# Attention of the first stage: probabilities turned in full precision, values as a narrow stationary operand in four column strips, scores in row halves

## The reference, cut to what matters

```python
qp = (q @ Wq + bq).reshape(B, H, S, hd)      # H = 16 heads, hd = 16, q = layernorm(x)
kp = k @ Wk + bk                             # one key and one value head for all 16
vp = v @ Wv + bv                             # k = v = ctx, 77 rows
att = softmax(einsum('bhsd,btd->bhst', qp, kp) / 16)
out = einsum('bhst,btd->bhsd', att, vp)      # back to [B, S, 256]
x = x + tanh(g) * out
```

## Time and profile before

| | us |
|---|---|
| median of 3 runs | 1150.58 (1150.38 to 1151.35) |
| the profiled execution | 1147.46 |
| its span, first to last instruction | 1145.7 |
| mean granted TensorE clock | 0.939 |

### The profile page before, as it was taken

One profiled execution on the slowest core, in us unless ns is written; L12 is line 12 of the kernel. 1 busy time (PEld: TensorE's weight loads), 2 busy tenths in 40 slices (PEclk: granted clock), 3 DMA queues, 4 the chain that ended last, 5 costly groups with the idle time before them and its releaser, 6 DMA issues. The chain is left out here.

```text
span 1145.7 us, 24403 instructions
## 1 busy us (share of the span) xinstructions
PE 981.6 (86%) x7085; PEld 868.5 (76%) x7085; DVE 855.9 (75%) x2301; ACT 588.9 (51%) x1349; POOL 489.0 (43%) x695
## 2 busy tenths in 40 slices
PE   5889989989998675899999999982779869999973
PEld 3767777777776443799999999972668769999962
DVE  3788998898996343688888888875666747888767
ACT  2577777777776352334343434422545346666520
POOL 3455455455453001345354444433376714444420
PEclk9899999999998776999999999996889989999996
DMA  6674674575560040101011010200333213444357
GB/s 157 148 139 96 141 143 96 122 142 116 112 143 1 0 128 22 49 25 48 24 35 37 24 48 24 93 2 1 101 125 120 89 55 117 125 123 130 106 200 241
DMA packets 85875, 104.44 MB, mean 91 GB/s; under 512 B 15070, under 2 KB 75438, under 8 KB 85808
## 3 DMA queue, kind: packets, MB, share of 16 engines
q1 hardware_dynamic: 77616, 81.91, 28.9%
q0 software_dynamic: 7632, 21.05, 5.1%
q10 hardware_dynamic: 560, 0.66, 0.2%
HBM read 38.50 MB, written 57.62 MB: 84 GB/s over the span
## 5 line engine op out<-in xcount | busy, mean ns | idle before, releaser
L413 POOL TENSOR_TENSOR prob_lo_hi<-prob,prob_lo_hi 128x616 f16<-128x616 f32 x64 | 95.7, 1496 | 126.7 <-ACT prob_lo_hi L491 126.5
L1647 POOL DMA_INDIRECT expert_out<-early_weights,aim x71 | 69.9, 984 | 101.3 <-DVE aim L1976 84.1
L721 PE MATMUL ps_scores<-kblock,qT 128*128 128x308 f32 x256 | 82.8, 448 | 11.1 <-ACT qT L475 5.8
L1638 POOL DMA_INDIRECT sorted_rows<-m_z,slot_i x64 | 72.5, 1133 | 42.4 <-DVE slot_i L1856 24.6
L1185 ACT ACTIVATE f_hidden<-c_hidden,f_b 128x256 f32<-128x256 f32 x128 | 53.7, 471 | 69.3 <-PE c_hidden L1374 69.3
L1372 PE MATMUL c_mlp<-f_w_hi,f_hidden_hi 128*128 128x256 f32 x256 | 80.9, 316 | 3.6 <-DVE f_hidden_lo L1303 3.6
L787 PE MATMUL ps_probT<-ident,prob_lo_hi 128*77 128x128 f32 x512 | 68.9, 279 | 15.4 <-DVE probT L364 12.8
L787 PEld LDWEIGHTS ps_probT<-ident,prob_lo_hi 128*77 128x77 f32 x512 | 59.3, 151 | 28.6 <-DVE probT L364 16.5
L1372 PE MATMUL c_hidden<-y2T_hi,f_w_hi 128*128 128x256 f32 x256 | 77.7, 304 | 0.0
L629 DVE TENSOR_REDUCE mx<-ps_scores 128x8 f32<-128x616 f32 x64 | 50.6, 791 | 32.8 <-PE ps_scores L721 32.8
L1374 PE MATMUL c_hidden<-y2T_hi,f_w_lo 128*128 128x256 f32 x256 | 72.8, 284 | 0.0
(11 more groups left out here) (336 smaller groups left out, 3306.3 us busy)
## 6 DMA issues: line engine op xcount, KB each, us to landing
sorted_rows<-no_row SPq DMA_DIRECT2D x15, 2322.0 KB, 13.4
m_z<-sorted_rows SPq DMA_DIRECT2D x71, 129.0 KB
early_weights<-expert_chunks SPq DMA_DIRECT2D x8, 640.0 KB, 4.2
combT<-combineT_all SPq DMA_DIRECT2D x16, 256.0 KB, 2.3
slT<-slots_all SPq DMA_DIRECT2D x16, 256.0 KB, 2.5
early_weights<-expert_out SPq DMA_DIRECT2D x8, 512.0 KB, 6.3
early_weights<-expert_out POOLq DMA_DIRECT2D x8, 512.0 KB, 6.3
out<-x_all SPq DMA_DIRECT2D x8, 512.0 KB, 3.4
```

The lines of the kernel that those rows point to most:

```text
L413: pool.tensor_tensor(prob2[:, u % 2, :, :, 0], prob[:, u % 2], prob2[:, u % 2, :, :, 1], ALU.subtract).then_inc(lo_done.sem, 1)
L721: return pe.matmul(out, lhsT, rhs, start=start, stop=stop)
L1638: pool.indirect_dma_start(out=sorted_rows[:, :], in_=zn[:, s % 3, t, :], in_offset=None, out_offset=bass.IndirectOffsetOnAxis(ap=slot_i[:, ...
L1647: pool.indirect_dma_start(out=expert_out[:, :], in_=xo[:, i % 3, :], in_offset=None, out_offset=bass.IndirectOffsetOnAxis(ap=aim_i[:, i % ...
```

## The change: what it does

- The probabilities are no longer split. `high_part` and `low_part` go; `turn_p` transposes the fp32 probabilities themselves. `scores_out` now waits for `turn_p` to have read the buffer, where it waited for `low_part`.
- `values` is turned round: the stationary operand is `vstat`, [77, 32] (16 values, a column of ones, 15 of zeros), and a pair of heads with all 256 tokens moves (512 columns, fp32). Four such matmuls put their 32 output rows at partitions 0, 32, 64 and 96 of one bank. There are two steps, of 8 heads each, in the place of four. `v_load` (POOL) adds the bias and fills `vstat`; `v_parts` and `add_bv` go.
- The result stands with the head's values down the partitions, so it is copied out (`values_out`, ACT, two of [128, 512]) and transposed back (`turn_values`, PE, two of four transposes). `out_rec` and `out_scale` (DVE) then read PSUM, once per tile of tokens; `out_sum` goes.
- `scores` uses 64 rows a matmul: the upper half of `qT` with `kblock`'s upper rows, then the lower half with the lower rows. `kblock` has 4 heads of columns (308) in place of 8, with a mask that is made once (`hmask`).
- `kv` streams 77 and 16 columns in place of 128 and 128.
- `probT_out` of unit 0 moves from DVE to ACT (`probT_act`, 0).
- DVE's first waits and the mask's construction ahead of the loop grow by one small POOL operation ([128, 4]).
- `order` is another list; the stages of the steps stay, and `v_load` is in MID.

```diff
-        kblock = sb("kblock", [P, UG, L])
-        vpart = sb("vpart_all", [L, NB, 3, HD + 1], BF16)
+        kblock = sb("kblock", [P, UG // 2, L])
+        vall = sb("v_all", [L, NB, HD])
+        vstat = sb("v_and_one", [L, 2 * HD])
+        turned = sb("values_turned", [P, 2, 512])
...
+        order = [(PRE, "ln1_stats"), (OUT, "probT_act", 3), (OUT, "turn_p", 3), (MID, "scores", 0), (OUT, "values", 0),
+                 (MIX, "turn_xu"), (PRE, "ln1_mean"), (MID, "row_max", 0), (MID, "scores_out", 0), (OUT, "values_out", 0),
+                 (MIX, "xuT_out"), (OUT, "values", 1), (PRE, "ln1_apply"), (MID, "row_max", 1), (MID, "scores", 1),
+                 (MIX, "neg_max"), (OUT, "out_rec", 0), (OUT, "values_out", 1), (MID, "exps", 0), (MIX, "combine"),
+                 (MID, "exps", 1), (MID, "scores_out", 1), (MIX, "dispatch"), (MIX, "combineT_out"), (MIX, "logits"),
+                 (OUT, "turn_values", 0), (OUT, "out_scale", 0), (MIX, "neg_maxT"), (MIX, "logitsT"),
+                 (OUT, "turn_values", 1), (MID, "scores", 2), (OUT, "out_rec", 1), (OUT, "out_scale", 1),
+                 (MIX, "normalise"), (MIX, "disp_scale"), (MID, "probT_act", 0), (MIX, "turn_comb"), (MID, "row_max", 2),
+                 (MID, "scores_out", 2), (OUT, "x1"), (MID, "turn_p", 0), (PRE, "kv"), (MIX, "comb_scale"),
+                 (PRE, "kv_move"), (OUT, "ln2_stats"), (MID, "row_max", 3), (MIX, "turn_disp"), (MID, "scores", 3),
+                 (MIX, "disp_out"), (MID, "exps", 2), (OUT, "ln2_mean"), (MID, "turn_p", 1), (MID, "probT_act", 1),
+                 (PRE, "zT_out"), (PRE, "turn_z"), (MID, "scores_out", 3), (OUT, "ln2_center"), (MID, "exps", 3),
+                 (MIX, "slots_out"), (MIX, "slot_inputs"), (OUT, "squares"), (PRE, "rstd1"), (PRE, "q_out"), (OUT, "unit"),
+                 (OUT, "ln2_scale"), (MID, "turn_p", 2), (MID, "probT_out", 2), (OUT, "rstd2"), (MID, "v_load"),
+                 (OUT, "runit"), (PRE, "kv_out"), (PRE, "queries")]
...
             tile, g0 = u // 2, (u % 2) * UG
+            if u % 2 == 0:
+                reuse(eng, pv_mm, b, tile + 1)
...
+            def v_load(b):
+                need(pool, v_out, b)
+                reuse(pool, pv_mm, b)
+                pool.tensor_tensor(vstat[:, 0:HD], at2(vall, b), bvt[0:L, 0, :], ALU.add).then_inc(v_in.sem, 1)
...
+            def values_out(b, w):
+                need(act, pv_mm, b, w + 1)
+                reuse(act, back_mm, b)
+                act.copy(turned[:, w], (psA[:], psB)[w]).then_inc(vt_ev.sem, 1)
...
+            def per_head(tile):
+                return (psA[:], psB)[tile].rearrange("p (h d) -> p h d", h=G)
+
+            def out_rec(b, tile):
+                need(dve, back_mm, b, tile + 1)
+                dve.reciprocal(orec[:, tile, :], per_head(tile)[:, :, HD]).then_inc(o_step.sem, 1)
...
             def kv(b):
                 need(pe, ctx_in, b)
-                reuse2(pe, osum_done, b)
+                reuse2(pe, o_step, b)
                 for k in range(KD):
-                    mm(psA[:, 0:P], wk[:, k, :], ctxT[:, k, :], k == 0, k == KD - 1)
+                    mm(psA[:, 0:L], wk[:, k, :], ctxT[:, k, 0:L], k == 0, k == KD - 1)
                 for k in range(KD):
-                    last = mm(psA[:, P:2 * P], ctxT[:, k, :], wv[:, k, :], k == 0, k == KD - 1)
+                    last = mm(psA[0:L, P:P + HD], ctxT[:, k, 0:L], wv[:, k, 0:HD], k == 0, k == KD - 1)
...
                 for h in range(2):
-                    last = mm(psS[:, h, 0:UG // 2 * L], qT[:, chunk, tile * P:(tile + 1) * P],
-                              kblock[:, h * UG // 2:(h + 1) * UG // 2, :].rearrange("p g l -> p (g l)"))
+                    rows = slice(h * P // 2, (h + 1) * P // 2)
+                    last = mm(psS[:, h, 0:UG // 2 * L], qT[rows, chunk, tile * P:(tile + 1) * P],
+                              kblock[rows].rearrange("p g l -> p (g l)"))
...
             def turn_p(b, u):
-                need(pe, lo_done, b, u + 1)
+                need(pe, exp_done, b, u + 1)
...
-                pairs = prob2[:, u % 2].rearrange("p g l two -> p g (l two)").bitcast(F32)
                 for g in range(UG):
-                    last = pe.transpose(psT[0:L, g, :], pairs[:, g, :], ident[:])
+                    last = pe.transpose(psT[0:L, g, :], prob[:, u % 2, g, :], ident[:])
...
             def values(b, w):
+                need(pe, pt_ev, b, 2 * w + 2)
                 if w == 0:
+                    need(pe, v_in, b)
+                heads = probT[:].rearrange("k (w i j) t g -> k w j i (t g)", w=2, i=2)
+                for j in range(4):
+                    last = mm((psA[:], psB)[w][j * 2 * HD:(j + 1) * 2 * HD, :], vstat[:], heads[:, w, j])
                 last.then_inc(pv_mm.sem, 1)
+
+            def turn_values(b, tile):
+                need(pe, vt_ev, b)
+                for w in range(2):
+                    for i in range(2):
+                        n = 2 * w + i
+                        last = pe.transpose((psA[:], psB)[tile][:, n * P:(n + 1) * P],
+                                            turned[:, w, i * S + tile * P:i * S + (tile + 1) * P], ident[:])
+                last.then_inc(back_mm.sem, 1)
```

More of the change, by code:

```diff
@@ L308, in phase_a @@
         PRE, MID, OUT, MIX = range(4)
[L310 to L330, removed]
@@ L451, in runit @@
                 pool.tensor_tensor(ru[:], ru[:], self.minus_half[:, 0:TT], ALU.pow).then_inc(ru_step.sem, 1)
-            run(pool, order, dict(rstd1=rstd1, add_bv=add_bv, low_part=low_part, v_parts=v_parts, rstd2=rstd2, runit=runit), NB)
+            run(pool, order, dict(rstd1=rstd1, v_load=v_load, rstd2=rstd2, runit=runit), NB)
         @block.scalar
@@ L562, in _ @@
             run(act, order, dict(kv_move=kv_move, zT_out=zT_out, q_out=q_out, exps=exps, probT_act=probT_act, unit=unit, disp_scale=disp_scale,
[L563 removed]
+                                 values_out=values_out, squares=squares,
                                  xuT_out=xuT_out, combine=combine, dispatch=dispatch, combineT_out=combineT_out,
@@ L591, in kv_out @@
                 reuse(dve, sc_mm, b)
-                dve.scalar_tensor_tensor(out=kblock[:], in0=spread(kT[:].rearrange("p (a l) -> p a l", a=1), 1, UG),
-                                         scalar=bk[:, 0:1], in1=spread(gmask[:].rearrange("p (g a) -> p g a", a=1), 2, L),
+                dve.scalar_tensor_tensor(out=kblock[:], in0=spread(kT[:].rearrange("p (a l) -> p a l", a=1), 1, UG // 2),
+                                         scalar=bk[:, 0:1], in1=spread(hmask[:].rearrange("p (g a) -> p g a", a=1), 2, L),
                                          op0=ALU.add, op1=ALU.mult).then_inc(kb_done.sem, 1)
@@ L713, in _ @@
             run(dve, order, dict(kv_out=kv_out, ln1_stats=ln1_stats, ln1_apply=ln1_apply, row_max=row_max, scores_out=scores_out,
-                                 probT_out=probT_out, out_sum=out_sum, x1=x1, out_rec=out_rec, out_scale=out_scale, ln1_mean=ln1_mean, ln2_mean=ln2_mean,
+                                 probT_out=probT_out, x1=x1, out_rec=out_rec, out_scale=out_scale, ln1_mean=ln1_mean, ln2_mean=ln2_mean,
                                  neg_maxT=neg_maxT, comb_scale=comb_scale, ln2_stats=ln2_stats, ln2_center=ln2_center, ln2_scale=ln2_scale,
@@ L788, in turn_p @@
                 last.then_inc(pt_mm.sem, 1)
             def values(b, w):
-                tile, half = w // 2, w % 2
-                bank = (psA, psB)[half]
+                need(pe, pt_ev, b, 2 * w + 2)
                 if w == 0:
-                    need(pe, pt_ev, b)
-                    need(pe, v_step, b)
-                if w >= 2:
-                    need(pe, osum_done, b, w - 1)
-                both = probT[:].rearrange("k h t g -> k h (t g)").bitcast(F16)\
-                               .rearrange("k h (q two) -> k h q two", two=2)
@@ L801, in values @@
-                W = 3 * (HD + 1)
-                rhs = at(vpart, b).rearrange("k c d -> k (c d)")
-                for h in range(8):
-                    for part in (1, 0):
-                        last = mm(bank[:, h * W:(h + 1) * W], both[:, half * 8 + h, tile * P:(tile + 1) * P, part], rhs,
-                                  part == 1, part == 0)
-                last.then_inc(pv_mm.sem, 1)
+                    need(pe, v_in, b)
+                heads = probT[:].rearrange("k (w i j) t g -> k w j i (t g)", w=2, i=2)
@@ L845, in slot_inputs @@
                 last.then_inc(sl_mm.sem, 1)
-            run(pe, order, dict(kv=kv, turn_z=turn_z, queries=queries, scores=scores, turn_p=turn_p, values=values,
+            run(pe, order, dict(kv=kv, turn_z=turn_z, queries=queries, scores=scores, turn_p=turn_p, values=values, turn_values=turn_values,
                                 turn_xu=turn_xu, logits=logits, logitsT=logitsT, turn_comb=turn_comb, turn_disp=turn_disp,
```

89 lines of the change are left out of this document (20 added, 69 removed).

## The result

The changed kernel takes 1107.67 us (median of 4, 1106.18 to 1109.23) against 1150.48 (1149.81 to 1151.35): ratio 0.9615, 95% interval 0.9591 to 0.9639. The profiled execution took 1107.69, its span is 1105.9. Forecast were 1125 and a range of 1108 to 1152: the direction and the loop were right, the size was not. The gain is 42.8 us where 25 were forecast.

The account below looks back on a forecast made before the run. PE's work and waits were taken as the bound: 19.3 + 0.5 = 19.8 us a turn against 21.68, -24 over 13 turns and -1 at the ends, so -25 from the median: 1125 us, range 1108 to 1152.

Parts of the forecast that it names:

- The bound: First stage: PE bounds the kernel, with 19.06 us of work and 2.62 of waiting in a 21.68 us turn.
- The terms of PE's sum: PE's work per loop turn: -2.08 + 1.75 - 1.80 + 1.71 + 0.87 - 0.19 = +0.26 us, from 19.06 to 19.3.
- ten changes of shape: PE's array switching between whole, row halves and strips: 0.175 us each, +1.75 a turn, bounds 0 to +3.0.
- Row halves and four strips: `scores` halves fully overlap, -2.08 us a turn; four `values` strips run at once, +1.71 for both steps.
- The three waits: PE's waits for the copy and `xu` go, that of `scores` 0 for `q_out` stays at 0.25; all waits 0.5 us.
- The first three and last three turns: Partly filled turns at the stage's ends: -1 us in all, bounds +2 and -5.
- The loop's size: 13 loop turns of 19.8 us against 21.68, -1.85 each: -24 us.
- the dip of the clock: One loop turn's half-rate stretch, clock 0.94 over 30 us, lost 1.8 us; no more expected, only widening the own case.
- Slow strips: `values` strips overlap little: about 1198 us one after another, 1175 with staggered records; together chance 0.13.
- two strips at a time: `values` runs only two strips at once: +1.7 us a turn, about 1148 us; chance 0.06.
- waits that stay: Late `unit` or `probT_act` holds PE for 2 us a turn as before: 1150 to 1154 us; chance 0.05.
- cheap changes of shape: Most of the 0.175 us per change hides behind work: -1 us a turn more, 1110 us; chance 0.12.

Follow-up runs that it names:

- run 6: Changed kernel with `turn_z` twice, with `ln2_center` twice, or with seven matmuls for four per `values` step: turns 20.19, 19.75 and 24.87 us, against 19.75.
- Run 4: Changed kernel's steps in the old kernel's order, unit 0's copy back on DVE: 1153.41 us, turn 21.99 us.
- run 3: Kernel before with both casts left out and `values` working on a constant, order as before: 1147.57 us, turn 20.92 us.
- runs 1, 2 and 4: In order: changed kernel with casts back in the chain, 1221.54 us; kernel before with three moves of the new order, 1188.45; changed steps in old order, 1153.41.
- run 7: Filler transposes or matmuls on PE at the stage's ends: kernel before 1145.51 us; changed kernel 1109.97 (last turns) and 1106.25 (both ends), without fillers 1115.12.
- e13: Changed kernel as it is, traced a second time on another chip as the yardstick: 1115.12 us, ratio to the kernel before 0.9609.
- e10: Kernel before with filler transposes on PE in its third turn and its last turns: 1145.51 us.
- e4: Changed kernel with `turn_z` done twice, four more transposes on PE: turn 20.19 us, against 19.75.
- e9: Changed kernel with `ln2_center` done twice, more work on DVE: turn 19.75 us, against 19.75.
- e5: Changed kernel with filler transposes on PE in the last two turns: 1109.97 us, ratio to the kernel before 0.9593.
- e12: Changed kernel with fillers on PE in the last two turns and ahead of the stage's first waits: 1106.25 us, ratio to the kernel before 0.9550.

## Why the prediction was right or wrong

**The bound: right.** PE bounds the loop after the change (probes of run 6), and it was PE's work plus waits before.

**The terms of PE's sum: right.** (What the prediction calls eight matmuls of `logits` are eight records of four matmuls; the sum counts records and is not touched by it.) Forecast +0.26 a turn of work. Measured: of the turn's 19.75, 0.39 is the wait of `scores` 0 for `q_out` (1.26 between `turn_p` 3 and it, less 0.87) and 0.20 that of `turn_disp` for `disp_scale`. The second shows only in ACT's row, which ends at 184.39, while `turn_disp` starts at 184.44:

```profile
183.48 0.91 ACT L473 ACTIVATE dispT<-dispT,erec 128x256 f32<-128x256 f32 x2
184.44 0.33 PE L701 MATMUL ps_turned<-ident,dispT 128*128 128x128 f32 x1
```

So PE's work is 19.16, against 19.06 before: +0.10. The matmuls of the turn without anything around them are 17.48 (six groups of transposes 0.435, `values` 2 x 0.86, `scores` 4 x 0.52, four groups of eight at 1.73, `turn_p` 4 x 0.875, `kv` 0.65), which leaves 1.68 for ten changes of shape: 0.17 each, forecast 0.175. Changes from and to the whole array, which no row had shown, cost what those between halves did: from `turn_values` 1 at 180.96 over `scores` 2 and `turn_comb` to `turn_p` 0 at 182.70 it is 1.74 us, the three groups alone are 0.435 + 0.52 + 0.435, and the other 0.35 are one change into the halves and one back. Row halves and four strips overlap in full, as taken. `kv` gained 0.24 (taken 0.19): its first group takes 0.41, its second 0.24 where the next step does not wait. Run 4 shows it, from 177.09 to the next step at 177.33:

```profile
177.09 0.39 PE L738 MATMUL ps_small_a<-consts_attention,ctx_turned 128*77 128x16 f32 x4
177.33 0.31 PE L804 MATMUL ps_probT<-ident,prob 128*77 128x128 f32 x1
```

**The three waits: right.** Those for the copy and for `xu` went, that for `q_out` stayed at 0.39 (forecast 0.25) and that for `disp_scale` came with 0.20 (0.1); all waits are 0.59 (0.5). `ln2_scale` took 0.88 (taken 1.0), and the rows at run 3 show the reason that was argued, POOL's `low_part`. What the prediction did not say, and runs 1, 2 and 4 showed, is that neither the new steps nor the moves of the order win anything in the loop without the other: the old order puts each producer right before its reader, and with the casts in the chain the new one makes PE wait up to 3.2 us for the copy. Leaving out the casts by itself does take one wait away, the one for the copy (run 3, 0.8 us a turn), as long as the steps are the old ones.

**The failed step: "The first three and last three turns ... I give them -1 (bounds +2, -5)".** They gave -11.2. This one term is 10.2 of the 17.8 us missed. It was named with its causes, the steps, the low clock and the casts in the chain, and given a size that no sum stood behind. What the runs showed in its place, in estimates from rows of single traces:

*Ahead of the loop, -6.2.* The third turn gives 3.5 of it. 1.3 are the clock's: the kernel before has a half-rate stretch there and the changed one has none (run 7). That leaves 17.4 of its 18.8; the new steps in the old order take 17.2 (run 4) and the changed kernel 15.3, so 0.2 are the steps' and 1.9 the order's. The casts alone give none (run 3: 18.7). Another 2.5 lie between the end of that turn and the first `turn_xu`, where the new order has one `turn_p` and two waits less, and 0.2 at the start.

*Behind the loop, -5.0.* From `turn_xu` to `turn_xu` and to phase b the pieces go from 20.22 to 18.18, from 20.09 to 17.82 and from 16.73 to 16.03. The first of them holds almost a full turn's steps, nearly all at full clock, and saves 2.0, as much as a full one. The second seems to save as much, but with fillers it takes 16.38 before and 17.43 after, of which 0.9 is the fillers' own delay: what it saved was the clock's. With fillers in both kernels the whole part is 51.4 against 48.7; without the half-rate stretch of 1.6 in the one and the delay of 0.9 in the other that is 49.8 against 47.8. So about 2 of the 5.0 are work and waits, and about 3 the clock's.

In all some 4.4 of the 11.2 are the low clock, which cost the kernel before more than the changed one, and the rest is order and steps. That is the division of this pair of traces: in the second trace of the changed kernel (e13) the part behind the loop is 2.3 us longer, by the half-rate stretches alone. The prediction counted 13 turns and left out that the next one is nearly full too; its own 1.85 would have given -1.9 more there. How the 1.9 behind the loop divide between order and steps stays open.

**The loop's size.** The 13 turns gave 3.2 more than forecast. 1.94 a turn for 1.85 is 1.2 of it, and 1.6 is the dip of the clock that the kernel before had once in its loop and the changed one not; the other 0.4 are rounding and a first and a last turn that are a little shorter. The prediction named the dip and gave its absence nothing. 3.0 are the profile's distance from the median, taken over to the forecast; 1.4 came in phases b to d, which no run explains.

**The rivals.** Slow strips, two strips at a time, waits that stay, cheap changes of shape: all refuted by the turn of 19.75 and its 0.17 a change. The Trainium skill (TensorE: Matmul & The Clock Gate, Part 3, "The mechanism") states that matmuls start and end in program order. If the two records of each matmul also stood behind one another, a `values` step would take five slots of 0.43; the trace has two bunches of four records, each bunch starting within 0.1 us. So the trace refutes the five slots; it agrees with the rule itself only if the records of the four matmuls are interleaved, first the four first ones and then the four second ones.

## What to carry to other kernels

Price a software pipeline by all its turns: those at the ends that hold most of the steps save what a full turn saves (2.0 us here for the one behind the loop), and where PE waits there, the low clock is a term of its own (about 4.4 of the 11.2 us here). When a change drops a step from a chain, ask at once which order becomes possible: here the new steps alone (+0.3 us a turn) and moves of the order alone (+2.2) lost, and together they won 1.94. Filler matmuls into a free bank, in the few long waits of PE at both ends, kept the clock up there and gave 8.9 us more; they must end before what PE waits for is ready, where 48 of them ended 0.9 us too late. And a run meant to price the clock must be read for what its fillers delay and for dips that fall elsewhere: in e10 these hid 1.3 us of the clock's cost in the third turn and 1.6 in the last part.

## What the runs showed that was not expected

- In the first 20 us the clock column says 1.00 in every trace, yet the eight records of `queries` take 3.37 to 3.78 us there without fillers and 1.99 with them. In the changed kernel it says 1.00 from 20 to 40 us too, where `turn_p` takes 1.99 in place of 1.05. A matmul's duration tells the rate where the column does not.
- The kernel before had a half-rate stretch in its loop at 214.8 us (clock 0.94 in the earlier trace rows), with fillers at its ends at about 193.3. The six traces of the changed kernel with PE 99% busy (plain twice, the probes e4 and e9, e5 and e12 with fillers) have none between 60 and 339 us.
- Matmuls with 77 and 16 moving columns take 0.10 and 0.06 us a record (0.41 and 0.24 for four), where 128 columns take 0.11: 16 columns are an eighth of 128 and cost more than half as much. What sets the time of the narrow ones no run shows.
